# Eight one-hot compares of a round as one wide compare, in a message-passing graph network

## What is computed

```python
x = x + L0(h, src, dst)     # in the reference the normalised features, scaled, summed over the edges
n = ln(mlp(node_feat)); e = ln(mlp(edge_feat))                    # encoders, width 64
for s in range(2):
    ce = concatenate([e, n[senders], n[receivers]])
    e = e + ln(mlp(ce))                                           # edge step
    agg = segment_sum(e, receivers)
    n = n + ln(mlp(concatenate([n, agg])))                        # node step
return mlp(n)                                                     # decoder, added to x
```

## Time and profile before

| | |
|---|---|
| Time, median of 3 runs | 13,500.32 us (13,497.44 to 13,505.08) |
| Profiled execution, first to last instruction | 13,501.9 us, 1.6 us over the median |
| Busy share: TensorE / GpSimd / ScalarE / VectorE | 75% / 67% / 55% / 42% |
| First gather of the first layer to its last | 865 to 4,863 us |
| First to last gather of the two edge steps | 5,128 to 9,140 us and 9,315 to 13,320 us |

### The profile page before, as it was taken

The page is one execution under the profiler, slowest core; times in us unless marked ns, Lnnn a source line. Parts: engine busy times, 40 slices in busy tenths (PEclk is TensorE's granted clock), DMA queues, the critical chain, the costliest instruction groups (busy, mean ns, idle before and its releaser), DMA issues. The chain is left out here.

```text
span 13501.9 us, 245430 instructions
## 1 busy us (share of the span) xinstructions
PE 10188.2 (75%) x61106; PEld 7311.0 (54%) x61106; DVE 5621.3 (42%) x18295; ACT 7395.3 (55%) x11725; POOL 9021.1 (67%) x9433
## 2 busy tenths in 40 slices
PE   4877777777777777777777777777777777777777
PEld 3655555555555555555555555554555555555554
DVE  5653333333333334444444444443444444444443
ACT  0025555555555535666666666665666666666665
POOL 0037777777777736777777777773777777777773
PEclk9986666666666658999999999998999999999998
DMA  2012222222222223333333333332222333333331
GB/s 76 11 27 43 43 43 43 42 43 43 43 43 43 43 33 82 93 94 94 94 94 94 94 94 93 94 94 58 68 68 68 68 68 68 68 69 68 68 69 33
DMA packets 1693848, 867.49 MB, mean 64 GB/s; under 512 B 1234324, under 2 KB 1391253, under 8 KB 1693347
## 3 DMA queue, kind: packets, MB, share of 16 engines
q1 hardware_dynamic: 1390930, 589.01, 16.6%
q0 software_dynamic: 301056, 257.50, 11.7%
q10 hardware_dynamic: 1808, 20.32, 0.5%
HBM read 635.66 MB, written 246.07 MB: 65 GB/s over the span
## 5 line engine op out<-in xcount | busy, mean ns | idle before, releaser
L1151 POOL DMA_INDIRECT edge_blk_g<-sender_part,edge_blk_idx x6272 | 6014.8, 959 | 2441.7 <-issue 1997.8
L892 POOL DMA_INDIRECT fl_g<-sender_x,fl_idx x3136 | 2992.8, 954 | 1025.9 <-issue 992.3
L1203 PE MATMUL edge_blk_hps<-ident,edge_blk_g 128*128 128x128 f32 x6272 | 1081.6, 325 | 1635.5 <-DMA edge_blk_g<-sender_part,edge_blk_idx 1635.3
L1203 PEld LDWEIGHTS edge_blk_hps<-ident,edge_blk_g 128*128 128x128 f32 x6272 | 910.5, 223 | 2284.9 <-DMA edge_blk_g<-sender_part,edge_blk_idx 2284.0
L1231 ACT ACT_TABLE_LOAD x1568 | 2011.7, 1283 | 51.6 <-PEq L66 23.6
L1276 DVE TENSOR_TENSOR edge_blk_t<-edge_blk_yb,edge_blk_rps 128x512 f32<-128x512 f32 x784 | 539.5, 688 | 2420.5 <-PE edge_blk_rps L1167 2420.3
L1237 ACT ACTIVATE edge_blk_h<-edge_blk_hps,vecs 128x512 f32<-128x512 f32 x784 | 538.8, 687 | 1485.5 <-PE edge_blk_hps L1203 1483.1
L1244 ACT ACTIVATE edge_blk_sq<-edge_blk_yps,vecs 128x512 f32<-128x512 f32 x784 | 538.9, 687 | 1388.7 <-PE edge_blk_yps L1211 1384.1
L984 ACT ACTIVATE fl_sq<-fl_yps,vecs 128x512 f32<-128x512 f32 x392 | 269.4, 687 | 1641.2 <-PE fl_yps L947 1641.2
L1308 DVE TENSOR_SCALAR edge_blk_ohb<-row_f,edge_blk_lst 128x64 f32<-128x64 f32 x6272 | 1115.7, 277 | 6.4
L975 ACT ACT_TABLE_LOAD x784 | 1005.9, 1283 | 31.5 <-PEq L66 17.5
(11 more groups left out here) (222 smaller groups left out, 15503.1 us busy)
## 6 DMA issues: line engine op xcount, KB each, us to landing
edge_blk_e<-edge_state SPq DMA_DIRECT2D x784, 256.0 KB
edge_state<-fl_e SPq DMA_DIRECT2D x392, 256.0 KB
edge_blk_dlb<-local_dst SPq DMA_DIRECT2D x1568, 64.0 KB
edge_blk_g<-sender_part,edge_blk_idx POOLq DMA_INDIRECT x6272
edge_state<-edge_blk_new SPq DMA_DIRECT2D x392, 256.0 KB, 2.1
fl_g<-sender_x,fl_idx POOLq DMA_INDIRECT x3136
edge_blk_win<-receiver_part SPq DMA_DIRECT2D x1568, 16.0 KB
fl_attr<-attr_slots SPq DMA_DIRECT2D x392, 32.0 KB
```

What stands on the lines that cost most here:

```text
L892: pool.indirect_dma_start(out=g[n.b][:, j, :], out_offset=None, in_=xg_d, in_offset=bass.IndirectOffsetOnAxis(ap=idx[n.b][:, j:j + 1].bitc ...
L1151: pool.indirect_dma_start(out=g[n.b][:, i, 64 * c:64 * c + 64], out_offset=None, in_=ps_d, in_offset=bass.IndirectOffsetOnAxis(ap=idx[n.b] ...
L1203: ins = nc.tensor.matmul(h_ps[:, P * i:P * i + P], g[n.b][:, i, :], ident[:, :], start=False, stop=i == TILES - 1)
```

## The change

The eight compares of a tensor with a column become one compare of two tensors. The first operand is `row_f[:, 0:64]` repeated over the eight blocks, the second is `lst` with each of its eight columns repeated 64 times. The output is the whole of `ohb`, 128x512. The waits before and the semaphore behind it are the same. It is made in both places, in `first_layer` and in `edge_step`.

```diff
--- before.py
+++ after.py
@@ -1034,10 +1034,9 @@
                         return
                     landed(dve, list_in, n)
                     wait(dve, sum_ok, n.back(2))
-                    for j in range(8):
-                        ins = v.tensor_scalar(ohb[n.b][:, j, :], row_f[:, 0:WIN], lst[n.b][:, j:j + 1].bitcast(F32), None,
-                                              ALU.is_equal)
-                    ins.then_inc(oh_ok, 1)
+                    v.tensor_tensor(ohb[n.b][:, :, :], row_f[:, 0:WIN].rearrange("p (j w) -> p j w", j=1).broadcast_to([P, 8, WIN]),
+                                    lst[n.b][:, :].bitcast(F32).rearrange("p (j w) -> p j w", w=1).broadcast_to([P, 8, WIN]),
+                                    ALU.is_equal).then_inc(oh_ok, 1)
 
                 def body(n):
                     wait(dve, turned, n)
@@ -1304,10 +1303,9 @@
                         return
                     landed(dve, list_in, n)
                     wait(dve, sum_ok, n.back(2))
-                    for j in range(8):
-                        ins = v.tensor_scalar(ohb[n.b][:, j, :], row_f[:, 0:WIN], lst[n.b][:, j:j + 1].bitcast(F32), None,
-                                              ALU.is_equal)
-                    ins.then_inc(ohb_ok, 1)
+                    v.tensor_tensor(ohb[n.b][:, :, :], row_f[:, 0:WIN].rearrange("p (j w) -> p j w", j=1).broadcast_to([P, 8, WIN]),
+                                    lst[n.b][:, :].bitcast(F32).rearrange("p (j w) -> p j w", w=1).broadcast_to([P, 8, WIN]),
+                                    ALU.is_equal).then_inc(ohb_ok, 1)
 
                 def body(n):
```

## The result

| | before | after |
|---|---|---|
| Time, median | 13,500.0 us (13,497.4 to 13,505.1, 4 runs) | 13,607.1 us (13,599.7 to 13,620.5, 4 runs) |
| Ratio | | 1.0079, interval 1.0065 to 1.0093 |
| Span of the profiled execution | 13,501.9 us | 13,597.9 us |
| VectorE busy | 5,621 us | 4,873 us |
| Gathers busy / idle before them, all 9408 | 9,007.6 / 3,467.6 us | 9,108.8 / 3,467.5 us |

A forecast was written before the change was run, and what follows sets the result against it. The prediction took GpSimd's gather queue, never running dry, as the bound. Its terms, 75 + 6 + 14 - 7 - 2 = 86 us on the 13,500 us median, gave 13,586 us; range 13,488 to 13,680.

The forecast's parts named there:

- The bound: In all three loops GpSimd's gather queue never runs dry: about 12,000 of the 13,502 us.
- What VectorE gets back: Per round, a 0.69 us compare returns about 0.73 us to VectorE, worth nothing on the path.
- A long instruction with two SBUF tensors holds a gather until its end: At the wide compare, gathers stand until it ends: held once, chance 0.60, 86 us slower in sum.
- Nothing is held: Rival: gathers beside the new compare have no excess, 13,491 us; chance 0.24.
- The window: A 0.69 us compare holds a gather if it starts between 0.56 and 0.10 us before it.
- the term of 75 us: Edge steps: 374 of 784 compare series start in the window, mean hold 0.20 us, adding 75 us.
- that of 6.5 us: First layer: 38 of 392 compare series start in the window, mean hold 0.17 us, adding 6.5 us.
- a bound of 0: Window's late edge at 0 instead of 0.10 us before the gather: 110 to 180 us added.
- The moved L1316: Edge steps: held gathers come later against L1316's 784 starts, adding 14 us.
- Small terms: Taken off: 7 us of gathers held by the old short compares, 2 us at the three loops' drains.
- Two in a row: Rival: gather held by L1282 stays held through the new compare, 151 us more, about 13,715 us; chance 0.12.
- Faster: Rival: L1282's 38 us belong to the compares after it, which give them back, 13,453 us; chance 0.04.

The follow-up runs named there:

- e9_wide_split8: Changed kernel's wide compare, row in SBUF, with L1282, L1316 and L1019 cut in eight pieces: 17,029.3 us where the kernel before takes 17,065, ratio 0.9976.
- e6_short_tt: Kernel before, its eight 128x64 compares each made with two SBUF tensors, one a repeated column: 17,057.1 us where the kernel before takes 17,027, ratio 1.0018.

## Why the prediction was right, point by point

- *The bound.* Right. GpSimd's idle time didn't move, and the span follows the gathers' busy time in four kernels.
- *What VectorE gets back.* Right: 0.69 us for the compare and nothing gained on the path; the time turned into the three waits shown. VectorE's busy time fell by 749 us where 860 was forecast: by the groups the compares did lose 859 us, but the eight short ones had overlapped their neighbours, and L1316 takes 525 ns now, where it took 496.
- *A long instruction with two SBUF tensors holds a gather until its end.* Right, and shown by the PSUM operand. *Nothing is held* falls. Of the two sentences of the Trainium skill ("SBUF — State Buffer", Who interferes with whom) the first agrees: the compare with two SBUF inputs blocked the gathers, which take their indices from SBUF, by up to 0.54 us. The second, the inference that tensor_tensor leaves descriptor generation alone, gave the wrong forecast here; whether these gathers stand while their indices are read or in descriptor generation, no run shows.
- *The window.* Its late edge was mis-sized. I had read 0.10 us before the gather off L1282. In the profile of before L1282 holds from 0.11 us on and not at 0.09; the compare holds from 0.03 us on in the edge steps and from 0.05 in the first layer. Why the two differ wasn't tried. 37 us of the edge steps' excess and 5.5 of the first layer's are from compares that start later than 0.10 us before. They make the term of 75 us 108, and that of 6.5 us 13; the prediction had this case, a bound of 0, in the upper end of its range.
- *The moved L1316.* Wrong in sign: forecast +14 us, measured -20 (51.0 to 30.7). My shift held each later gather against unchanged starts of L1316; why its excess fell instead, and rose to 58 us in the doubled compare, wasn't tried.
- *Small terms.* The short series' 7 us were 5.9; L1282 and L1019 gave 2 and 4 back; the 2 us of the drains are too little to be seen. The terms: +104.5 + 11.2 - 2.0 - 20.3 - 4.1, and 11.8 that stand beside other lines or in gathers less than 30 ns over the median, make 101.1 us; 8.7 of these 11.8 are the median's step from 944 to 945 ns, which is no hold and was in no term. So 86 us against 107 was nearer than its parts, by luck: the compares' terms were 42 us too low and L1316's 34 too high.
- *Two in a row* didn't come: no gather of the changed kernel is over 1.482 us, and the doubled compare shows the release. Behind a short piece it does come, as e9_wide_split8 shows. *Faster* falls with the compares' 4 us: L1281 has 35.4 us beside it still.

## What to carry to other kernels

If GpSimd's queue of indirect DMAs never runs dry, a long VectorE instruction that reads two SBUF tensors (0.69 or 0.75 us here), or a long one like L1316 and L1019 (one SBUF tensor, 512 elements in some 0.5 us), costs gather time, though VectorE is at 42%. Then read the spread between a gather's median and mean first. One operand in PSUM took the compare's hold away, short pieces took away most of the others', and fewer and longer instructions bring it back. Where another engine sets the pace the sign can differ: the edit in the edge steps alone was 1.1 and 1.6% faster there, and the whole edit wasn't timed there.

## What I had not expected of the hardware

The kernel before takes 13,500 us in two sets of runs and 17,027 to 17,377 us in three. The median gather of the kernels profiled is 944 or 945 ns in the first and 944 to 947 in the others. TensorE's mean granted clock is 0.84 to 0.86 of full speed in the first and 0.75 to 0.76 in the others. There it also runs with gaps, as in this stretch of e6_short_tt, where it waits for nothing that the trace shows:

```profile
6620.84 0.22 PE L1189 MATMUL edge_blk_aggps<-edge_blk_ohb,edge_blk_new_t 128*64 128x64 f32 x1 [1.26 <-issue]
6622.27 0.22 PE L1189 MATMUL edge_blk_aggps<-edge_blk_ohb,edge_blk_new_t 128*64 128x64 f32 x1 [1.22 <-issue]
6623.68 0.26 PE L1189 MATMUL edge_blk_aggps<-edge_blk_ohb,edge_blk_new_t 128*64 128x64 f32 x1 [1.20 <-issue]
```

Such waits before this line are 451 us in e6_short_tt, while the kernel before shows none on the first chip. Which of gaps and clock brings the other, and what brings both, wasn't tried. Nor was why instructions can pass a waiting gather behind a short piece while behind a long one they don't, and whether the hold comes from the gather's read of its indices; that is only argued.
